# Moving the second score pair of an attention step behind that step's fill work

## The reference

```
x: (4, 1024, 256)   ctx: (4, 77, 256)
h = layernorm(x)
q, k, v = h Wq, h Wk, h Wv            16 heads of 16
A = (q k^T / 4)^2, lower triangle     (the chunked form of the reference is this, summed)
x += (A v / (rowsum(A) + 1e-5)) Wo
s = layernorm(x); D = pairwise distances of ctx rows and s rows
path = cheapest monotone path through D (dynamic programming, then traced back)
x += for each token, the sum of the ctx rows that the path pairs with it
f = layernorm(x)
h = butterfly(f W_exp + b_exp, up_weights)      10 stages, each pairs channels 2^stage apart
h = butterfly(gelu(h + up_bias), down_weights)
x += h W_con + b_con + down_bias      (the kernel folds both butterflies into the two matrices)
```

## Time and profile before

| | us |
|---|---|
| median of three runs | 844.45 |
| profiled execution, device time | 842.61 |
| its span, first to last instruction | 840.9 |
| TensorE matmul busy | 763.6 (91%) |
| VectorE busy | 481.7 (57%) |
| ScalarE busy | 438.4 (52%) |
| GpSimd busy | 146.2 (17%) |
| TensorE clock granted, mean | 0.961 of full |

### The profile page before, as it was taken

The page is one execution under the profiler, slowest core; times in us unless marked ns, Lnnn a source line. Parts: engine busy times, 40 slices in busy tenths (PEclk is TensorE's granted clock), DMA queues, the critical chain, the costliest instruction groups (busy, mean ns, idle before and its releaser), DMA issues.

```text
span 840.9 us, 12176 instructions
## 1 busy us (share of the span) xinstructions
PE 763.6 (91%) x3991; PEld 384.6 (46%) x3991; DVE 481.7 (57%) x1928; ACT 438.4 (52%) x664; POOL 146.2 (17%) x331
## 2 busy tenths in 40 slices
PE   5878999789999997999999989887999995999998
PEld 4453333234433354333334333444486584558567
DVE  6636655544446323399999999455999885040000
ACT  1136876766788755697777788423312300440220
POOL 2120322311322211122322223022000000200200
PEclk9899999989999998899999999979999996999999
DMA  4383325302224320134340332101010112001001
GB/s 158 136 239 129 124 82 160 113 1 75 82 76 158 122 69 23 24 92 129 114 150 25 92 100 46 18 9 24 25 50 29 28 49 52 12 1 38 13 14 37
DMA packets 53162, 61.29 MB, mean 73 GB/s; under 512 B 21407, under 2 KB 32339, under 8 KB 53099
## 3 DMA queue, kind: packets, MB, share of 16 engines
q1 hardware_dynamic: 49835, 54.22, 21.4%
q0 software_dynamic: 1088, 4.19, 1.6%
q10 hardware_dynamic: 2176, 2.10, 0.7%
HBM read 37.17 MB, written 23.32 MB: 72 GB/s over the span
## 4 chain that ended last, share of the span: by engine, by line
PE 59%; DVE 22%; ACT 8%; issue 5%; DMA 4%; SPq 2%; ACTq 0%; DVEq 0%
PE psO L1317 13%; PE psS L1300 12%; PE psW L1481 7%; PE psS L1466 7%; PE psW L1369 5%; ACT ARENA L873 4%; DVE FOLD L1021 4%; PE psW L1392 3%; DVE FOLD L1081 2%; PE psW L1376 2%; PE psW L1456 2%; PE psW L1401 2%; SPq L629 2%; DVE FOLD L1019 2%; DMA qk_parts<-ARENA 2%
## 5 line engine op out<-in xcount | busy, mean ns | idle before, releaser
L873 ACT ACTIVATE ARENA<-psS 128x1024 f32<-128x1024 f32 (+3 forms) x384 | 299.8, 812 | 105.7 <-PE psS L1300 102.5
L1300 PE MATMUL psS<-ARENA 96*128 96x512 bf16 (+3 forms) x768 | 188.1, 335 | 23.4 <-ACT ARENA L873 22.3
L793 POOL TENSOR_SCALAR_AFFINE_SELECT ARENA<-ARENA 128x256 f32<-128x256 f32 x256 | 110.0, 434 | 388.0 <-ACT ARENA L873 385.7
L1317 PE MATMUL psO<-ARENA 128*32 128x512 f32 (+3 forms) x1536 | 168.6, 512 | 0.8 <-ACT ARENA L878 0.8
L1300 PEld LDWEIGHTS psS<-ARENA 96*128 96x128 bf16 x768 | 56.2, 99 | 203.7 <-ACT ARENA L873 124.1
L1481 PE MATMUL psW<-W2E,ARENA 128*128 128x256 f32 x512 | 113.8, 379 | 0.4 <-ACT ARENA L893 0.4
L1481 PEld LDWEIGHTS psW<-W2E,ARENA 128*128 128x128 f32 x512 | 96.9, 189 | 14.8 <-ACT ARENA L893 0.6
L949 ACT ACTIVATE ARENA<-psS,BEFF 128x512 f32<-128x512 f32 x64 | 43.4, 687 | 90.1 <-PE psS L1466 90.1
L1369 PE MATMUL psW<-XX,ARENA 128*128 128x512 f32 x128 | 68.6, 638 | 3.0 <-DVE ARENA L1180 3.0
L1192 DVE TENSOR_TENSOR X<-X,psW 128x512 f32<-128x512 f32 x32 | 21.5, 680 | 78.4 <-PE psW L1456 39.5
L1466 PE MATMUL psS<-XX,MIXA 128*128 128x512 f32 x128 | 58.8, 614 | 3.7 <-ACT ARENA L949 2.7
(11 more groups left out here) (146 smaller groups left out, 813.5 us busy)
## 6 DMA issues: line engine op xcount, KB each, us to landing
ARENA<-qk_parts SPq DMA_DIRECT2D x192, 128.0 KB, 2.7
qk_parts<-ARENA SPq DMA_DIRECT2D x16, 768.0 KB, 3.5
X<-in_x POOLq DMA_DIRECT2D x3, 1024.0 KB, 6.0
dist<-ARENA SPq DMA_DIRECT2D x1, 2560.0 KB, 7.8
MORE<-dist SPq DMA_DIRECT2D x16, 160.0 KB, 2.2
out<-ARENA ACTq DMA_DIRECT2D x8, 256.0 KB, 2.1
out<-ARENA SPq DMA_DIRECT2D x8, 256.0 KB, 2.1
path<-MORE SPq DMA_DIRECT2D x16, 80.0 KB, 2.0
```

The lines of the kernel that those rows point to most:

```text
L793: pool.affine_select(out=blk, in_=blk, compare_op=ALU.is_ge, fill=0.0, base=0, pattern=[[0, 2], [1, P]], channel_multiplier=-1).then_inc(s ...
L873: nc.scalar.activation(A[:, (2 * G + a) % A_PAIRS, :, 0:N], psS[:, a, :, 0:N], ACT.Square).then_inc(s_sq, 1)
L1300: ins = nc.tensor.matmul(psS[:, a, j, 0:N], KST[0:STACK, g % 2, 2 * a + j, kt * P:(kt + 1) * P], QST[0:STACK, g % 2, 2 * a + j, q0:q0 + N] ...
L1317: ins = nc.tensor.matmul(psO[32 * j:32 * j + 32, o % 2, q0 - qc * HALF:q0 - qc * HALF + N], V1[:, kt, GH * g + j], A[:, (2 * G + j // 2) % ...
```

## The change

A new function `seconds_behind_fill` rewrites the finished list. A second score pair (a = 1) of any step but a batch's first is taken out, held, and put back directly in front of the next unit that is a scores or a products unit. Everything else keeps its place. So a step that read "first pair, products, second pair, fill" becomes "first pair, products, fill, second pair", and the second pair now stands directly in front of the first pair of the next step. In a batch's last step it stands in front of the products of step 46. All engines follow the new list: on ScalarE the square of the second pair comes behind that fill's reads and roots, and on GpSimd its mask comes behind the fill's pieces.

```
+def seconds_behind_fill(plan):
+    out, held = [], []
+    for u in plan:
+        if held and u[0] in ("scores", "products"):
+            out, held = out + held, []
+        if u[0] == "scores" and u[3] == 1 and u[2]:
+            held = [u]
+        else:
+            out.append(u)
+    return out + held
...
     plan += hidden(3, 0) + hidden(3, 1) + outs(3, 0) + outs(3, 1)
+    plan = seconds_behind_fill(plan)
     plan = flat([u, ("gelu",) + u[1:]] if u[0] == "hidden" and u not in early_hidden else [u] for u in plan)
```

## The result

The changed kernel took 851.59 us, median of six runs (849.79 to 852.26); the kernel before, on the same chip, 843.39 (838.18 to 844.98). The ratio is 1.0108, with an interval of 1.0073 to 1.0144: 8.2 us slower. The forecast of 849 us, slower but within 1%, had the direction and nearly the size; the measured 1.08% lies just past the 1% it named. Its terms were wrong, and the rest of this document is about them.

What follows compares the result with a forecast made beforehand. TensorE was taken as the bound, matmuls in flight 91% of the span. Terms 6.4 + 1.7 - 3.3 + 1.3 - 1.0 = +5.1 us on 842.61 gave 847.7, or 849.6 from the median; forecast 849 us, range 839 to 859.

Steps and rivals of the forecast that it cites:

- TensorE's own cost of the new order: Changeovers between matmul groups, the only new neighbour being products then fill: price 0, bounds 0 and 10.9 us.
- weights behind the products: Rival, chance 0.07: float32 weight loads stand open behind products, 121 x 0.09 us on top of the sum, 859 us.
- Steps without matmul fill: Back-to-back score pairs give ScalarE two squares at once, the second late for the next first pair: +6.4 us, bounds 2.9 and 18.
- the 31 runs: Runs of steps without matmul fill: 6 priced at 0.58 us each, 12 at 0.24, 13 in narrow steps at 0.
- ScalarE held by something with its own date: Second pair's square queues behind a root or read that waits for VectorE or a transfer: +1.7 us, bounds 0 and 4.
- the distance tile of the earlier trace: Step 31 of batch 3, where ScalarE reads a distance tile: TensorE's wait forecast to grow from 1.33 to about 1.9 us.
- What the change wins: Second pairs that wait and have matmul fill behind them: 13 waits x 0.25 = -3.3 us, bounds -5.5 and -1.
- the four starts: Four of the 13 waiting second pairs, at batch starts: gains expected to come back in part as the next first pair's wait.
- the weight folding of batch 0: Line 930, four places alike where ScalarE is full in either order; given as reason for the upper bound of 4 us.
- Fills that wait: Pairs that ran while fills waited for VectorE now run after, +0.44 us each, three counted: +1.3 us, bounds -3 and +4.4.
- The side queues: GpSimd's masks behind the fill's pieces and SyncE's operand transfers: each priced 0.
- The clock: Rival, chance 0.14: longer TensorE gaps bring half-clock stretches, each 6.8 us more costing 3.4; 852 to 857 us.

Runs made afterwards that it cites:

- the seven pairs: Only seven second pairs moved (batch 0 steps 42 to 44; batch 1 steps 1, 13; step 1 of batches 2, 3), against the kernel before: 836.65 us, ratio 0.992.
- the four: Only second pairs at steps 1 and 13 of batch 1 and step 1 of batches 2 and 3 moved, against the kernel before: 841.54 us, ratio 0.9995.

## Why the prediction was right and wrong

**TensorE's own cost of the new order: priced 0, measured 8 to 9 us.** This is the step of the prediction that failed. The earlier trace rows compare the time from the products' start to the next start, 0.57 us in both, and the new kernel confirms exactly that: 196.68 to 197.67 and 245.89 to 246.88 are 0.99 us, as products to scores are 1.00 in the earlier trace rows. The cost sits one step later, between the fill's first and second matmul, and I had cut the comparison off in front of it. The upper bound that I had worked out, 121 x 0.09 = 10.9 us from the two load durations of the earlier trace rows, was the right mechanism and nearly the right size: 73 ns on each of 124 groups. The trace of the kernel before even held the price: its only value fill behind products was one of the rows I quoted, and it was never compared over its whole length with one behind wide scores. The Trainium skill (TensorE: Matmul & The Clock Gate, Weight-path perf modes) gives float32 weights no fast load; the runs agree, 189 ns against 99, and this rule had pointed the right way. The rival "weights behind the products" had 0.07; it should have been the forecast. Its time of 859 was too high, because it was put on top of a sum of waits that did not come.

**Steps without matmul fill: +6.4 forecast.** The mechanism is there, the count is wrong. Batch 3, the steps of the earlier trace rows, in the changed kernel:
```profile
476.59 1.03 PE L1315 MATMUL psS<-ARENA 96*128 96x512 bf16 x4
477.55 1.06 PE L1332 MATMUL psO<-ARENA 128*32 128x512 f32 x8
478.55 1.28 PE L1315 MATMUL psS<-ARENA 96*128 96x512 bf16 x4
479.75 1.06 PE L1332 MATMUL psO<-ARENA 128*32 128x512 f32 x8
480.75 1.04 PE L1315 MATMUL psS<-ARENA 96*128 96x512 bf16 x4
```
The 1.28 comes in an earlier pair of pairs, as forecast, but the next has 1.04: the wait moved up, and a run of two steps pays it once, as it did before. I had added the new one and not struck out the old. Only 19 of the 31 runs are single steps, and many of those are narrow.

**ScalarE held by something with its own date: +1.7 forecast.** Near the root:
```profile
84.19 1.73 PE L1315 MATMUL psS<-ARENA 96*128 96x512 bf16 x4 [2.52 <-ACT ARENA L888]
```
The wait now stands ahead of a second pair and is no longer than the 2.68 us of the earlier trace rows; from start to start in the records it is 2.68 and another 0.30 at the first pair behind, against 2.84 before. The square behind the hold delays the next first pair, but only by what TensorE has not meanwhile spent on the four score matmuls. At the distance tile of the earlier trace rows:
```profile
505.55 0.60 PE L1315 MATMUL psS<-ARENA 96*128 96x512 bf16 x2 [1.44 <-ACT ARENA L888]
506.47 0.87 PE L1315 MATMUL psS<-ARENA 96*128 96x512 bf16 x2 [0.31 <-ACT ARENA L888]
```
1.44 + 0.31 = 1.75 us against 1.33, where I had said about 1.9. Here the square did cost, 0.4 us. From the products' starts these steps lost 2.1 us in all, with a half-clock stretch at 506.7 to 510.1 that was not there before.

**What the change wins: -3.3 forecast.** At the four starts 2.4 us were won (0.49, 0.23, 1.26 and 0.44 by the starts of the products), the 1.26 with the clock as shown above. At the first of them, that of the earlier trace rows, products at 193.27 and the next at 196.57 lay 3.30 us apart before; the rows of the changed kernel above have products at 196.68, and those in front of them at 193.86: 2.82 us. Around the weight folding of batch 0, which I had counted as even, it won 2.1 us more, though half-clock stretches lie differently there as well. In the sum the scores' waits are unchanged, 35.4 us and 35.4: what the first two terms brought, these gains took back. **Fills that wait: +1.3** forecast, 18.5 to 19.7 us measured. The side queues, priced 0, show nothing.

**The clock.** It was a rival at 0.14 and was true in part. Half-clock stretches in the attention part take 44.2 us against 37.4, worth 2.0 us by the records and 3.4 if TensorE had streamed through all of them. Some went (the 10.2 us at 333.4 are 3.4 us now, -3.1 us), others came. One that came:
```profile
529.94 0.61 PE L1315 MATMUL psS<-ARENA 96*128 96x512 bf16 x2 [1.78 <-ACT ARENA L888]
530.85 1.03 PE L1315 MATMUL psS<-ARENA 96*128 96x512 bf16 x2 [0.30 <-ACT ARENA L888]
531.81 1.94 PE L1332 MATMUL psO<-ARENA 128*32 128x512 f32 x8
533.68 4.67 PE L1407 MATMUL psW<-WOP,ARENA 128*128 128x256 f32 x12
```
```profile
530.60:537.40 6.80, 6.55 (x19) 3.34 (x20) 0.11 (x1) 2.12 (x3) 0.00 (x0) 0.50 0.01 3
```
The twelve `wo` matmuls take 4.67 us at clock 0.50; before they took 2.75, behind a wait of 1.71 us instead of 1.78 and 0.30. The kernel before had such a place in the same group (seven in 3.32 us at 319.90, shown above) that is gone now, so the two leave the group's mean nearly alone. The mean clocks of the six runs are 0.960 to 0.966, and the profiled run before had 0.961: the clock does not carry the result.

So a forecast within 3 us was right by luck: 5 us of waits were counted that cancelled, and 8 us of loads were left out.

## What to carry to other kernels

Price a new neighbour over the whole of the group that follows it: compare up to the start of what comes behind, since a weight load that has lost its cover shows in the gap to the second matmul and leaves the first start where it was. In this kernel float32 fills cost 4 or 5 ns behind scores of 256 columns or more and 0.06 to 0.1 us behind the narrow tiles of the products, and 120 such small prices came to 9 us. Subtract the matmuls' own pace before a gap is called a cost. Move a unit only where it waits now and nothing that holds the other engine's queue follows, and move it on every engine that shares the order: all 188 moves lost 8.2 us, and one engine alone lost 20. The seven that were chosen so won 6.5 us, but most of that came with a higher clock; before a gain at one place is put down to the move, look at the clock there in a second kernel with the same order.

## What the runs showed of the hardware

The cover that a float32 load of 128 columns needs is visible in steps. With a fill of 256 columns, whose matmuls otherwise start 216 ns apart, the second starts 220 ns after the first behind scores of 256 columns and more, 272 behind scores of 128 columns (eight places, the same in three kernels), and 320 behind products. The fills that begin behind products stand behind float32 weights in tiles of 32 columns each time, so no run tells which trait of the products takes the cover away. For bf16 scores behind products and float32 fills behind products the first start is the same to 2 ns (525 and 523 ns from the last products' start at 512 columns), though their loads take 99 and 189 ns: a start in the record does not wait for the whole load.

Stretches at half clock (1.2 in place of 2.4 GHz) stand behind single gaps of 2.5 us and more, but also behind 1.78 and 0.30 us (529.94 in the changed kernel) and behind 0.90, 0.42 and 0.31 us (319.90 in the one before). At the first place 1.71 us brought none. At the second, 0.90 and 1.23 us brought none with the seven pairs, and 0.90 and 1.24 us brought one with the four: the gaps directly in front do not settle it. Nor does the program alone: the six runs of one program had clocks of 0.960 to 0.966.
